# Moving three normalisations of the attention input into the tail of the first FFN, in a fused FFN, attention, FFN kernel on 8 cores

## The reference

```python
x = x + 0.5 * ffn(layernorm(x))      # FFN1
x = x + attention(layernorm(x))      # 16 heads of 64, causal
x = x + 0.5 * ffn(layernorm(x))      # FFN2, same weights as FFN1

def ffn(h):        # top-2 of softmax(h @ W_gate), 7 gates, weights divided by their sum
    return h @ W_shared.T + (w0 + w1) * (h @ W_expert.T) + bias   # no token over capacity
```

## Time and profile before

| | us |
|---|---|
| median of two timed runs | 3725.91 (3723.62 and 3728.19) |
| profiled execution, its own time | 3752.8 |
| its span on the slowest core (core 1) | 3751.2 |
| spans of all cores | 3710.4 to 3751.2 |
| PE busy in it | 2252.3 |
| DVE busy | 1264.7 |
| ACT busy | 839.6 |

### The profile page before, as it was taken

How to read it: one execution, slowest core, us unless ns; L and a number is a source line. 1 busy time by engine, 2 the same in 40 slices (tenths; PEclk the granted TensorE clock), 3 DMA queues, 4 the chain that set the end, 5 groups by cost and what they waited for, 6 DMA issues and landing times.

```text
span 3751.2 us, 30894 instructions; the slowest of 8 cores (3710.4 to 3751.2 us)
## 1 busy us (share of the span) xinstructions
PE 2252.3 (60%) x8584; PEld 751.5 (20%) x8584; DVE 1264.7 (34%) x3292; ACT 839.6 (22%) x841; POOL 5.3 (0%) x31
## 2 busy tenths in 40 slices
PE   0076556766565565655556655676667656576557
PEld 0022122212221122211122212221222112221112
DVE  2243434224422145211344343422442223431114
ACT  0001300160005610056400130016100462003650
POOL 0000000000000000000000000000000000000000
PEclk9977678757886688877778757865776667777777
DMA  5501010100010000100010001000001000010000
GB/s 179 179 31 38 5 45 34 35 5 24 23 68 3 3 24 23 67 2 3 3 45 34 35 5 45 34 35 4 19 28 68 2 3 13 34 57 12 3 3 23
DMA packets 34939, 121.57 MB, mean 32 GB/s; under 512 B 4053, under 2 KB 14293, under 8 KB 28634
## 3 DMA queue, kind: packets, MB, share of 16 engines
q1 hardware_dynamic: 27866, 69.26, 5.4%
q10 hardware_dynamic: 6912, 50.33, 3.7%
HBM read 92.32 MB, written 23.07 MB: 31 GB/s over the span
## 4 chain that ended last, share of the span: by engine, by line
PE 34%; ACT 21%; DVE 21%; issue 13%; DMA 9%; DVEq 1%; ACTq 0%; SPq 0%; POOLq 0%
ACT PT L593 17%; PE PSA L582 5%; PE PSA L301 5%; PE PSA L443 4%; PE PSA L489 4%; PE PSA L465 3%; PE PSA L360 3%; PE PSA L365 3%; DMA XC<-x 2%; DVE JUNK L408 2%; ACT RGB L636 2%; DVE XC L411 2%; ACT SGR L633 2%; PE PSA L525 2%; DMA out<-XC 2%
## 5 line engine op out<-in xcount | busy, mean ns | idle before, releaser
L593 ACT ACTIVATE PT<-PSA,MBCC 128x2048 bf16<-128x2048 f32 x320 | 629.5, 1967 | 308.1 <-PE PSA L582 302.9
L301 PE MATMUL PSA<-IDE,XN 128*128 128x128 bf16 x768 | 185.1, 241 | 613.2 <-DVE XN L290 505.8
L623 PE MATMUL PSA<-PT,VB 128*65 128x512 bf16 (+3 forms) x1280 | 416.8, 468 | 170.2 <-DVE PT L602 141.6
L582 PE MATMUL PSA<-QT,KT 64*128 64x512 bf16 (+3 forms) x1280 | 248.6, 472 | 280.8 <-ACT PT L593 264.9
L360 PE MATMUL PSA<-WS_T,XNT 128*128 128x512 bf16 x1024 | 302.8, 449 | 164.6 <-DVE XC L411 136.5
L602 DVE TENSOR_TENSOR PT<-PT,TRI 128x128 bf16<-128x128 bf16 x512 | 115.1, 225 | 758.9 <-ACT PT L593 715.8
L365 PE MATMUL PSA<-WE_T,XNT 128*128 128x512 bf16 x1024 | 264.7, 405 | 0.0
L277 ACT ACTIVATE STAT<-STAT 128x1 f32<-128x1 f32 x96 | 19.5, 203 | 1016.5 <-DVE STAT L273 1016.5
L623 PEld LDWEIGHTS PSA<-PT,VB 128*65 128x65 bf16 x1280 | 147.8, 141 | 447.3 <-issue 412.7
L301 PEld LDWEIGHTS PSA<-IDE,XN 128*128 128x128 bf16 x768 | 77.1, 100 | 723.7 <-issue 723.7
L544 ACT COPY MBC<-PSA 128x16 f32<-128x16 f32 x8 | 1.4, 173 | 839.4 <-PE PSA L541 839.4
(11 more groups left out here) (92 smaller groups left out, 1659.9 us busy)
## 6 DMA issues: line engine op xcount, KB each, us to landing
WSTR<-wscr ACTq DMA_DIRECT2D x48, 1024.0 KB, 4.8
XC<-x SPq DMA_DIRECT2D x32, 512.0 KB
out<-XC SPq DMA_DIRECT2D x32, 512.0 KB, 2.7
wscr<-STGB SPq DMA_DIRECT2D x6, 1024.0 KB
STG<-wts SPq DMA_DIRECT2D x1, 4096.0 KB
STG<-wte SPq DMA_DIRECT2D x1, 4096.0 KB
STG<-wtp SPq DMA_DIRECT2D x1, 4096.0 KB
STG<-wtq SPq DMA_DIRECT2D x1, 4096.0 KB
```

The costliest lines, as they stand in the source:

```text
L301: last_pe = S.op("tensor", lambda e, slot=slot, dc=dc, pv=pv: e.transpose(pv, XN[:, slot, dc * 128:(dc + 1) * 128], IDE[:, :]), wait=(("s_ ...
L582: instr = e.matmul(bank(b, 512 - off, off), KT[hb:hb + 64, hp, j * 128:(j + 1) * 128], QT[hb:hb + 64, hp, off:512], start=True, stop=True)
L593: return S.op("scalar", lambda e, o=o, i=i: e.activation(o, i, AF.Exp, bias=MBCC[:, :]), wait=w, inc="s_sc")
L623: instr = e.matmul(PSA[0:65, ob(h) * 512 + off:(ob(h) + 1) * 512], VB[:, j, h, :], PT[:, sl, off:512], start=(j == 0), stop=(j == kend - 1))
```

## The change

The tail of FFN1 does more: for tiles 0, 1 and 2 it emits, behind pre(t), also the apply of attention's layernorm. The loop between FFN1 and Q then emits for these tiles the transposes and the copy alone; the apply of tile 3 is emitted behind the copy of tile 0. Nothing else changes: the same instructions with the same shapes, the same lists on PE, ACT, SP and POOL. Lines of the kernel behind L761 have numbers 8 to 15 higher afterwards.

```diff
         def mk_tail(g, ln):
             nxt = ln_next[ln]
             if nxt is not None:
+                if nxt == 1:
+                    def attn_tail(t, dv_ms):
+                        h = get_lnh(g, 1)
+                        h["pre"](t)
+                        if t < 3 and t not in h["applied"]:
+                            h["applied"][t] = True
+                            h.setdefault("ap", {})[t] = h["apply"](t, h["exps"][t])
+                    return attn_tail
                 return lambda t, dv_ms: get_lnh(g, nxt)["pre"](t)
...
             if do_attn:
                 guard = S.cnt["s_dv"]
                 lnh2 = get_lnh(g, 1)
+                ap2 = lnh2.pop("ap", {})
                 for t in range(NT):
-                    lnh2["full"](t)
+                    if t in ap2:
+                        lnh2["transpose"](t, ap2[t])
+                        if t == 0 and 3 not in lnh2["applied"]:
+                            lnh2["applied"][3] = True
+                            ap2[3] = lnh2["apply"](3, lnh2["exps"][3])
+                    else:
+                        lnh2["full"](t)
```

## The result

The changed kernel takes 3643.38 us (median of 11 runs, 3636.58 to 3683.06), the kernel before 3727.12 us (median of 10). The ratio is 0.9766 (95% interval 0.973 to 0.9803). In some runs the cores of one die work for a part of the time at a lower granted clock; the medians take in all runs of their count, the ratios leave out those that this made over 1% longer. The forecast was 3640 us and 0.977, so 86 us gained; 84 were measured. As the interval reaches to both sides of 0.98, the timing shows the kernel faster, and leaves open whether by more than 2%.

What follows compares the result with a forecast made beforehand. No engine was taken to bound the kernel throughout; eight FFN1-attention borders each held a 21.06 us ladder of DVE and PE waits. Saving 8 x 10.8 = 86 us from the 3725.9 us median gave 3640 us (0.977), range 3614 to 3671.

Steps and rivals of the forecast that it cites:

- item 1: FFN1's tails of tiles 0 and 1: moved applies fit DVE's idle gap before the copy, cost 0.
- item 2: FFN1's tail of tile 2: the moved apply delays all behind it on DVE by 1.62 us a group, on the path.
- item 3: FFN1-attention border: transposes 0 and 1 start early, first Q matmul at 626.2 instead of 637.0, gaining 10.8 us a group.
- item 4: Start of Q: first weight half lands by 623.2, 3 us before the Q matmul, so weights do not delay it.
- Sum: Whole kernel: eight borders at 10.8 us each save 86 us, giving 3640 us, ratio 0.977.
- Rival A: Border and Q: clock rises early, Q starts at the upper level, 16 us more gained, 3624 us; chance 0.15.
- Rival B: Q, K and V: a third clock level in three more groups gives back 31 us, 3671 us; chance 0.20.
- Rival C: FFN1's tails of tiles 0 and 1: applies not hidden, costing 27 us, 3667 us; chance 0.03.
- Rival D: FFN1: tail waits make the clock fall, 20 us a group lost, 161 in all, 3801 us; chance 0.02.

Runs made afterwards that it cites:

- experiment 2: Changed kernel with the applies in the tails of tiles 0 and 1 done three times each: 3661.0 us, ratio to before 0.9817.
- experiment 3: Changed kernel with only applies 0 and 1 in the tails, applies 2 and 3 behind copy 0 in the border: 3644.5 us, ratio to before 0.9761.
- experiment 4: Changed kernel with apply 2 put into tile 3's gate chain, where DVE waits for ACT, instead of tile 2's tail: 3634.2 us, ratio to before 0.9749.
- version 6: Changed kernel with the edits of experiment 4 and experiment 5 together: 3618.3 us, ratio to the kernel before 0.9703.
- experiment 5: Changed kernel with transposes and copy 0 ahead of tile 3's statistics and apply 3 behind copy 1: 3628.7 us, ratio to before 0.9725.
- experiment 8: Version 6 with the next group's statistics one tile later in FFN2's tails, tile 3's in the next FFN1 behind copy 1: 3522.4 us, ratio to before 0.9457.

## Why the prediction was right

- **Applies 0 and 1 hidden in the tails** (item 1): right. ACT's answer took 0.82 us for 0.81, the gap left 0.56 of idle time for 0.49, and experiment 2 shows that the gap ends where the profile said: two applies more slipped by 1.37 for 1.35.
- **Apply 2 delays by 1.62** (item 2): right, 1.64 in the profile. Experiments 3 and 4 show that this delay was on the path. The prediction did not draw the conclusion that lay in its own numbers, that the change would be better without this part of it.
- **The border** (item 3): right to 0.03 us, 8.63 for 8.6. One detail was off: transposes 1 did not end at 2.4 GHz, the clock fell during them. It cost nothing, as PE waited 3.8 us behind them.
- **What is late next** (item 4): right. L443 was released by the last copy in all eight borders. The margin of 3 us for the weights held in the changed kernel (they landed 5.2 to 5.6 us after the last statistics, and Q began at 8.63) and was used up in version 6, where they were late once.
- **Sum**: 86 us forecast, 84 between the medians; in the profiles the stretch from tile 2's statistics to Q is shorter by 10.4 to 11.1 us in each group, 86.6 over the eight.
- **Rival A** (an early rise of the clock): wrong. In all eight borders of the changed kernel's profile the burst of sixteen transposes ran at 0.50 throughout, and Q's first block too. The row for it, a window of the border of group 1:

```profile
616.00:620.00 4.00, 2.01 (x8) 0.81 (x9) 0.71 (x2) 0.00 (x0) 0.00 (x0) 0.50 0.62 227
620.00:622.00 2.00, 2.00 (x6) 0.71 (x5) 0.00 (x0) 0.00 (x0) 0.00 (x0) 0.50 0.17 70
```

- **Rival B** (the third level gives part of it back): wrong. The level is there, in both kernels, in other groups each time, and costs Q, K and V 7 to 10 us where it comes, but the change did not bring more of it. Of the twelve profiled executions four show it (the kernel before, the changed one and those of experiments 3 and 5), on all four cores of one die or on both dies; the other eight, which all have applies moved into the tails, show it on no core. What sets it off was not tried.
- **Rival C**: shown wrong by experiment 2. **Rival D**: its trigger was real, its price of 20 us a group was not.

## What to carry to other kernels

When two engines hand a tile back and forth in a ladder, ask of each rung whether its input is there before the ladder begins, and give it to the engine in the last gap in which it waits anyway; half of the gain here came not from the instruction that was moved but from what it let the other engine start. A move is free only where its engine would have waited at that place anyway: the same 0.8 us instruction cost nothing in two tails and 1.64 us in the third, where it did not wait. And an instruction that waits for an answer or a load asked for a moment before should stand one step later in its list: that alone, at another place, was worth more than the change.

## What the runs showed of the hardware

- The transposes here did not hold TensorE's clock. Behind dense matmuls it fell from 1.00 to 0.50 some 4 us into sixteen of them (0.60 over 606 to 608 in the changed kernel), and a burst of sixteen at 0.50 did not raise it in any of the eight borders. Q's matmuls of 512 columns did in both kernels, some 3 to 6 us after they began. The Trainium skill, "TensorE: Matmul & The Clock Gate", section "What's actually happening", says that activity releases the clock; Q's matmuls agree with it, the bursts of transposes do not.
- A fall inside a dense stage lasted some 3 us and cost PE 1.6 us there: behind 3.37 us without a matmul, sixteen matmuls took 2.40 + 2.76 instead of 1.89 + 1.90. Little of it reached the time, as DVE was what the stage waited for (experiment 2). Behind 7.70 us without one, eight matmuls took 3.57, all at the low clock (experiment 8).
- A granted clock of 0.81, neither of the two levels, came in 4 of the 12 profiled executions, on all four cores of a die at least, and where it lasted for a whole stage of Q, K and V it made this stage 7 to 10 us longer. The Trainium skill, same page, section "Seeing it yourself", has a limiter at 13/16, which agrees with the number. It also has this limiter come once three cores of a die run dense matmuls and stay while they do; that does not fit here, as all eight cores run these stages, and in 8 of the 12 executions no core shows the level. What sets it off was not tried here.
